# A sort on one core: the product of the last payload columns goes from VectorE to GpSimd, and bucket one-hots are made two steps sooner

## What is computed

```python
h = emb
acc = emb
for _ in range(LAYERS):                       # 2
    h = jax.ops.segment_sum(adj_val[:, None] * h[adj_col], adj_row, num_segments=N)
    acc = acc + h
graph_item_embs = acc / (LAYERS + 1)
...
scores = select @ _l2norm(graph_item_embs).T
```

## Time and profile before

| | us |
|---|---|
| median of 3 runs | 3988.06 (3985.89 to 3988.77) |
| the profiled execution | 3990.2 |
| its span | 3988.2 (mean granted TensorE clock 0.794) |
| busy over the span: PE / PEld / DVE / ACT / POOL | 2638.1 / 2222.1 / 3011.5 / 830.1 / 2657.9 |

### The profile page before, as it was taken

The page is one execution under the profiler, slowest core; times in us unless marked ns, Lnnn a source line. Parts: engine busy times, 40 slices in busy tenths (PEclk is TensorE's granted clock), DMA queues, the critical chain, the costliest instruction groups (busy, mean ns, idle before and its releaser), DMA issues.

```text
span 3988.2 us, 79764 instructions
## 1 busy us (share of the span) xinstructions
PE 2638.1 (66%) x14097; PEld 2222.1 (56%) x14098; DVE 3011.5 (76%) x7238; ACT 830.1 (21%) x2728; POOL 2657.9 (67%) x2685
## 2 busy tenths in 40 slices
PE   4899889555566566566666556665556555565898
PEld 2676666455565555555555555555555555553454
DVE  8999999767777677777777677767677777677675
ACT  0999999200000000000000000000000000004554
POOL 1355555777777777777776777777777777775771
PEclk7899999777777776777778677778787787786999
DMA  1011111422222222222223222222222222234343
GB/s 37 3 4 3 3 3 3 110 53 54 55 54 54 54 55 55 55 55 55 55 55 103 62 55 55 56 56 56 56 55 55 55 55 55 54 81 140 95 139 139
DMA packets 165449, 228.71 MB, mean 57 GB/s; under 512 B 79020, under 2 KB 119084, under 8 KB 164908
## 3 DMA queue, kind: packets, MB, share of 16 engines
q0 software_dynamic: 102640, 162.39, 19.8%
q1 hardware_dynamic: 47856, 58.94, 4.8%
q10 hardware_dynamic: 14540, 3.70, 0.8%
HBM read 183.57 MB, written 41.35 MB: 56 GB/s over the span
## 4 chain that ended last, share of the span: by engine, by line
DMA 30%; POOL 27%; issue 19%; DVE 13%; PE 6%; ACT 2%; SPq 2%; ACTq 0%; DVEq 0%; POOLq 0%
POOL store L649 25%; DMA store<-in_L_rec_emb,store 16%; DMA store<-table,store 13%; PE bank L1707 2%; DVE store L1020 2%; DVE big L964 2%; PE bank L1650 2%; POOL store L676 1%; DVE store L972 1%; ACT big L723 1%; DVE big L980 1%; DVE big L1445 1%; SPq L496 1%; DVE store L1045 1%; DVE store L906 1%
## 5 line engine op out<-in xcount | busy, mean ns | idle before, releaser
L1650 PE MATMUL bank<-store,shared 128*128 x9792 | 1731.2, 351 | 1137.5 <-POOLq L634 790.5
L1650 PEld LDWEIGHTS bank<-store,shared 128*128 128x128 f32 x9792 | 1610.9, 258 | 1257.8 <-issue 1255.5
L1338 DVE TENSOR_TENSOR acc<-acc,bank 128x256 f32 x2448 | 1022.6, 418 | 799.7 <-PE bank L1650 780.5
L1288 DVE TENSOR_SCALAR shared<-bank,mlo,mval 128x256 f32<-128x256 f32 x2448 | 1324.0, 541 | 0.0
L649 POOL DMA_INDIRECT store<-in_L_rec_emb,store x1128 | 1065.4, 945 | 384.2 <-issue 326.0
L649 POOL DMA_INDIRECT store<-table,store x1128 | 1066.4, 945 | 370.0 <-issue 317.9
L739 ACT COPY mlo<-store 128x24 f32 (+1 forms) x102 | 21.5, 211 | 2793.0 <-PE bank L1650 1977.6
L723 ACT ACTIVATE big<-big 128x72 f32<-128x72 bf16 x1764 | 569.7, 415 | 0.0
L1550 PE MATMUL bank<-big,store 128*128 128x144 f32 x2352 | 480.2, 333 | 72.1 <-DVE store L972 17.3
L1550 PEld LDWEIGHTS bank<-big,store 128*128 128x128 f32 x2352 | 357.0, 206 | 192.8 <-ACT big L723 169.5
L604 POOL DMA_INDIRECT sorted_edges<-moved,block_to x167 | 311.2, 1863 | 57.1 <-issue 57.1
(11 more groups left out here) (265 smaller groups left out, 1439.4 us busy)
## 6 DMA issues: line engine op xcount, KB each, us to landing
store<-in_L_rec_emb ACTq DMA_DIRECT2D x3008, 0.5 KB
store<-in_L_rec_emb SPq DMA_DIRECT2D x3008, 0.5 KB
store<-table SPq DMA_DIRECT2D x3008, 0.5 KB
store<-table ACTq DMA_DIRECT2D x3008, 0.5 KB
scores<-store SPq DMA_DIRECT2D x48, 512.0 KB, 2.8
store<-in_L_rec_emb,store POOLq DMA_INDIRECT x1128
store<-table,store POOLq DMA_INDIRECT x1128
table<-acc SPq DMA_DIRECT2D x7, 896.0 KB, 10.6
```

What stands on the lines that cost most here:

```text
L1288: dve.tensor_scalar(onehot[:, u % SR, :], bank[7][:, 0:BUCKET], mlo[:, u:u + 1], mval[:, u:u + 1], ALU.is_equal, ALU.mult).then_inc(s_S[u ...
L1338: add = dve.tensor_tensor(acc[:, bass.ds(off, BUCKET)], acc[:, bass.ds(off, BUCKET)], bank[u % PR][:, 0:BUCKET], ALU.add)
L1650: last = pe.matmul(bank[u % PR][:, q * D:(q + 1) * D], onehot[:, u % SR, q * P:(q + 1) * P], msg_flat[:, bass.ds(offs[u], D)], start=True, ...
```

## The change

GpSimd takes over the product of the last columns, and now of three columns (CL = 5: columns 5, 6, 7), in all 147 steps: one product of 128 x 432 f32 per step. VectorE's product of two columns (128 x 288) goes, and ScalarE makes 5 columns, 10 activations, where it made 6. GpSimd's order is written out: in `scatter(g)`, the products of steps 2 to 6 of group g+1 come ahead of the scatters 1, 3, 4, 6 and 7; those of step 7 and of step 0 of group g+2 follow the ninth scatter, and that of step 1 of group g+2 follows the gate that waits for the landing. Ahead of the loop GpSimd makes the products of the whole first group and of two steps more. In the last full group's scatter the product of the very last step comes behind all 9 scatters. VectorE's `hot_columns` now also waits for GpSimd's product of four steps before, GpSimd's product for `hot_c` and for the free slot, and TensorE for GpSimd's product ahead of column 5.

Besides, `hot_buckets` is issued for the group after next at step 6 (it was for the next group at step 0), and TensorE's `edges_before` (line 1535) at step 6 for the group after next.

```diff
+    CL = CA - 1
+    BETWEEN = {1: 2, 3: 3, 4: 4, 6: 5, 7: 6}
...
+            def last_columns(g, s):
+
+                n, r = SG * g + s, s % Q
+                pool.wait_ge(s_hc, n + 1)
+                pool.wait_ge(s_pm, n + 1)
+                pool.tensor_tensor(at_c[:, r, CL:C, :, :],
+                                   hot_c[:, r, :, CL:C].rearrange("p n t -> p t n").unsqueeze(2).broadcast_to([P, C - CL, 2, LC]),
+                                   pays[:, bass.ds(n * C + CL, C - CL), :].unsqueeze(3).broadcast_to([P, C - CL, 2, LC]),
+                                   ALU.mult).then_inc(s_valg, 1)
+
+            def scatter(g, h, blocks=NK, skip=0, after=0):
...
                 for k in range(blocks):
+                    if after == 2 and k in BETWEEN:
+                        last_columns(g + 1, BETWEEN[k])
                     pool.indirect_dma_start(slots, bass.IndirectOffsetOnAxis(block_to[:, h, k:k + 1], 0),
...
+                if after == 2:
+                    last_columns(g + 1, SG - 1)
+                    last_columns(g + 2, 0)
+                elif after == 1:
+                    last_columns(g + 1, 2)
                 pool.wait_ge(s_free, g + 3)
                 pool.wait_ge(s_sct, 16 * (NK * g + blocks))
                 pool.tensor_tensor(gate[:, 2:3], gate[:, 1:2], gate[:, 1:2], ALU.add).then_inc(s_free, 1)
+                if after == 2:
+                    last_columns(g + 2, 1)
...
-            with pool.Fori(0, GR // 2) as i:
+            for s in range(SG):
+                last_columns(0, s)
+            last_columns(1, 0)
+            last_columns(1, 1)
+            with pool.Fori(0, GR // 2 - 1) as i:
                 for h in range(2):
-                    scatter(2 * i + h, h)
+                    scatter(2 * i + h, h, after=2)
+            scatter(GR - 3, 0, after=2)
+            scatter(GR - 2, 1, after=1)
             scatter(GR - 1, 0, NKL, FIRST)
...
-                for t in range(CA):
+                for t in range(CL):
...
                 dve.wait_ge(s_val, CA * n + CA)
+                ge(dve, s_valg, n - Q + 1)
...
-            def last_columns(g, s):
-
-                n, r = SG * g + s, s % Q
-                dve.wait_ge(s_hc, n + 1)
-                dve.tensor_tensor(at_c[:, r, CA:C, :, :],
...
                 for s in range(SG):
-                    if s == 0 and hot is hot_b:
-                        hot_buckets(g + 1)
-                    elif s == 3:
+                    if s == 6 and early:
+                        hot_buckets(g + 2)
+                    if s == 3:
                         edges_before(g + 1)
...
-                    last_columns(g, s)
...
-                    if t < CA:
+                    if t < CL:
                         pe.wait_ge(s_val, Q * CA + CA * n + t + 1)
-                    elif t == CA:
-                        pe.wait_ge(s_valv, n + 1)
+                    elif t == CL:
+                        pe.wait_ge(s_valg, n + 1)
...
             edges_before(0, kept[:, 0])
+            pe.wait_ge(s_rk, 1)
+            edges_before(1, kept[:, 1])
...
                     permute(g, s, h, SG)
-                    if s == 0:
-                        edges_before(g + 1, hot)
+                    if s == 6 and hot is not None:
+                        edges_before(g + 2, hot)
                     elif s == 4:
                         bucket_steps(g)
```

More of the change, by code:

```diff
@@ L380, in recommender_program @@
         s_val = sem("s_val")
-        s_valv = sem("s_valv")
+        s_valg = sem("s_valg")
         s_pm = sem("s_pm")
@@ L598, in opened @@
                 pool.tensor_tensor(gate[:, 0:1], gate[:, 1:2], gate[:, 1:2], ALU.add).then_inc(s_gate, 1)
-            def scatter(g, h, blocks=NK, skip=0):
+            def last_columns(g, s):
[7 more added lines that the diff above has]
+            def scatter(g, h, blocks=NK, skip=0, after=0):
                 opened(g, [(s_gev, g + 3), (s_to, g + 2)])
                 for k in range(blocks):
+                    if after == 2 and k in BETWEEN:
+                        last_columns(g + 1, BETWEEN[k])
                     pool.indirect_dma_start(slots, bass.IndirectOffsetOnAxis(block_to[:, h, k:k + 1], 0),
@@ L724, in payloads @@
                                               scale=what[:, bass.ds(n * C + t, 1)])
-                    last.then_inc(s_val, 1)
+                    last.then_inc(s_val, 1 + CA - CL if t == CL - 1 else 1)
             with act.Fori(0, GR // 2) as i:
@@ L974, in hot_partitions @@
                                   ALU.is_equal).then_inc(s_hp, 1)
-            def last_columns(g, s):
-                n, r = SG * g + s, s % Q
-                dve.wait_ge(s_hc, n + 1)
-                dve.tensor_tensor(at_c[:, r, CA:C, :, :],
-                                  hot_c[:, r, :, CA:C].rearrange("p n t -> p t n").unsqueeze(2).broadcast_to([P, C - CA, 2, LC]),
-                                  pays[:, bass.ds(n * C + CA, C - CA), :].unsqueeze(3).broadcast_to([P, C - CA, 2, LC]),
-                                  ALU.mult).then_inc(s_valv, 1)
             def edges_before(g):
@@ L1078, in targets, with sort_group @@
                 dve.tensor_tensor(block_to[:, h, 0:blocks], bank[7][:, 0:blocks], number[:, :], ALU.add).then_inc(s_to, 1)
-            def sort_group(g, h, width=LC, hot=hot_b):
+            def sort_group(g, h, width=LC, hot=hot_b, early=True):
                 for s in range(SG):
-                    if s == 0 and hot is hot_b:
-                        hot_buckets(g + 1)
-                    elif s == 3:
+                    if s == 6 and early:
+                        hot_buckets(g + 2)
+                    if s == 3:
                         edges_before(g + 1)
@@ L1148, in _ @@
             for g in range(KEPT - 1):
-                sort_group(g, g % 2, LC, kept[:, g + 1])
+                sort_group(g, g % 2, LC, kept[:, g + 1], g + 2 >= KEPT)
             with dve.Fori(KEPT // 2, GR // 2 - 1) as i:
@@ L1153, in _ @@
             sort_group(GR - 3, 0)
-            sort_group(GR - 2, 1, LCL)
+            sort_group(GR - 2, 1, LCL, early=False)
             dve.wait_ge(s_lat, 3)
@@ L1159, in _ @@
                 hot_partitions(GR - 1, s, 0)
-                last_columns(GR - 1, s)
                 if s == 0:
@@ L1567, in _, with sort_group @@
             edges_before(0, kept[:, 0])
-            def sort_group(g, h, hot):
+            pe.wait_ge(s_rk, 1)
+            edges_before(1, kept[:, 1])
+            def sort_group(g, h, hot=hot_b):
                 for s in range(SG):
                     permute(g, s, h, SG)
-                    if s == 0:
-                        edges_before(g + 1, hot)
+                    if s == 6 and hot is not None:
+                        edges_before(g + 2, hot)
                     elif s == 4:
@@ L1578, in _ @@
             for g in range(KEPT - 1):
-                sort_group(g, g % 2, kept[:, g + 1])
-            with pe.Fori(KEPT // 2, GR // 2) as i:
+                sort_group(g, g % 2, kept[:, g + 2] if g + 2 < KEPT else hot_b)
+            with pe.Fori(KEPT // 2, GR // 2 - 1) as i:
                 for h in range(2):
-                    sort_group(2 * i + h, h, hot_b)
+                    sort_group(2 * i + h, h)
+            sort_group(GR - 3, 0)
+            sort_group(GR - 2, 1, None)
             for s in range(LAST):
```

## The result

The changed kernel takes **4037.18 us** (median of 4 runs, 4034.49 to 4037.64) against 3988.01: **1.0123 times as long, 95% interval 1.0105 to 1.014**. I had forecast 3972.5 with a range of 3938 to 4013. The profiled execution took 4034.49 us.

The account below looks back on a forecast made before the run. VectorE was taken to bound the sort at 32.86 us a group, then GpSimd at 32.0 after the change: -14.6 us for 17 groups, -4 at the start, +3 at the end, -15.6 in all, 3972.5 us, range 3938 to 4013.

Parts of the forecast that it names:

- VectorE's term for the shared read: VectorE in the sort: waits for GpSimd's reads add 3.0 us a group to 28.2, making 31.2.
- Its own work: VectorE's work per sort group without its product and count waits: 28.2 us, from 32.86.
- The product's price: GpSimd's product of 432 elements in the sort: 1.25 us each, eight make 10.0 a group.
- the two estimates from the Trainium skill: GpSimd's product by the skill's pages: 1.13 or 1.49 us, the group 31.1 or 33.9 us.
- GpSimd as the bound: GpSimd bounds the sort after the change, at 32.0 us a group, VectorE 0.8 under it.
- ScalarE is no bound: ScalarE in the sort: 80 activations a group instead of 96 leave 26 us.
- Buckets sooner: Earlier bucket one-hots in the sort remove VectorE's waits for TensorE's counts: 6.4 us over 17 groups.
- Start: Up to the first opening gate: -5.8 from VectorE's ten steps and 1.8 of stalls, -4 us.
- The end: After the last group's late third product: first codes 6 us late, the rest 3 us late, +3 us.
- Slower: Rival: GpSimd's queue in the sort bounds above the old bound, from 1.36 us a product; 4012 us, chance 0.28.
- fast: Rival: VectorE still bounds the sort, at its lower work, with cheap products; 3949 or 3928 us, chance 0.18.
- Mutual waits: Rival: GpSimd and VectorE hold each other off in the sort; group 32.8 us, 3986 us, chance 0.12.

Follow-up runs that it names:

- a_fence: The changed kernel with a one-element GpSimd fill, and a wait for it, ahead of each of the six products that follow a scatter: 3965.39 us, ratio 0.9949.
- d_read: The kernel before plus five unused GpSimd products per group, behind scatters 0, 2, 3, 5 and 6: 4047.96 us, ratio 1.0154.
- d_idle: The kernel before plus five unused GpSimd products per group, in a row behind the landing gate, where no scatter runs: 4012.1 us, ratio 1.0064.
- hot_early: The kernel before with only the bucket one-hots and TensorE's counts two steps sooner: 3983.2 us, ratio 0.9985.
- b_last: The kernel before with one unused semaphore declared last of all: 3990.74 us, ratio 1.000.
- f_tail: a_fence with the last group's third product behind the first scatter of the last full group, not behind all nine: 3956.74 us, ratio 0.9918.
- b_sem: The kernel before with one unused semaphore declared ahead of those of the gather rounds: 3973.61 us, ratio 0.996.
- a_sem: The changed kernel with one unused semaphore where a_fence has its own, without fences: 4023.74 us, ratio 1.008.

## Why the prediction was wrong

**The step that failed is VectorE's term for the shared read**, 28.2 + 3.0 = 31.2 us. Its own work was right: 28.2 + 6.8 of measured holds = 35.0, which is its busy time a group (594.86 / 17); the last 0.6 of the 35.57 is its idle time. The prediction sized the holds at less than half, for two reasons. *The length of one*: it let a read wait for at most a product, 1.25 us. The rows show holds of 2.2, since a product already holds while it stands behind a scatter. a_fence takes away just that and wins 58 us, 3.4 a group, nearly the 3.8 that the term was short; the holds that it leaves, 2.8 a group, are about the 3.0 forecast. *How many*: it took products and reads as meeting by chance. They meet by schedule. The products wait for VectorE's own one-hots and are placed between scatters that run at one pace, so the same lines are hit in each group: line 1073 takes 2.38 to 2.44 us in 17 of its 19 runs.

Under both lies a premise of the text ahead of the prediction, that the engines "meet only at semaphores". d_read has no semaphore between its products and VectorE, and VectorE lost 4.3 us a group by them.

A third thing was missing: line 1073 (1054 before) reads one SBUF operand, and so was in no sum of the prediction. Held 2.1 us on average, it is the largest single item, 38 of the 122 us. The Trainium skill's same section of "SBUF — State Buffer" ("Who interferes with whom") warns of it: a `tensor_scalar` can enter a two-port mode, and then contends with GpSimd. The trace shows the contention (0.185 to 2.28 us), not the mode.

**The product's price** was a little high: 1.11 us for 1.25, so the strided operand cost little: a product of packed constants takes 1.06 (d_idle, 5.29 for five). The select's rate in the sum is 1.52 ns by its two rows and not 1.56, which moves the price by 0.02 us. Of the two estimates from the Trainium skill the lower, 1.13, came close; the surcharge for wide steps of its page "GPSIMD Engine Reference", section 7 (1.49 with it), did not show in 1.11.

**GpSimd as the bound**: wrong for the change (gate idle 34.8 us), right for the fenced kernel, where 32.0 forecast stands against 32.20. That nearness is in part luck: the fenced kernel has six fences a group that the sum has not (in the rows of a_fence the product starts at 599.14, 0.46 us behind the scatter's end at 598.68; the sum has 0.1), and its products are cheaper than priced.

**ScalarE, hot buckets, start, end.** ScalarE is no bound, as said. Buckets sooner: 6.4 forecast, 6.7 us in hot_early. Start -5.9 for -4: 1.8 of stalls had been added, and the gate came 5.9 sooner, near what VectorE's ten steps alone give (5.8); but b_last, whose sort is the same as before, has that gate 1.0 sooner too. The end +10.3 before and -5.6 after the first gather, +4.7 for +3: behind TensorE's last step the chain to line 1278 took 25.2 us (761.65 to 786.85) and not 21.1. In f_tail, undoing the late product alone, the last full group's gate to the first gather is 35.6 us again.

**The rivals.** *Slower* had the right sign and the wrong mechanism: it needed a product above 1.36 us, and it was 1.11. By the same 1.11 the *fast* rival should have won: VectorE did bound, as it says, but not at its lower work. *Mutual waits* named the cause and gave it 0.8 us a group more, 32.8; it was 35.57. The prediction says that no row shows a VectorE operation held by GpSimd, and let one last a product at most. What a trace doesn't show was here the whole result. The kernel before could not show it, for GpSimd ran nothing there but one-element sums and scatters. A bound with each of the six products that follow a scatter holding a read for both, and the other two for themselves, 6 x (1.55 + 1.25) + 2 x 1.25 = 19.3 us a group, would have put the range's end far above 4013.

## What to carry to other kernels

Work moved to an idle engine can be paid by the bounding one, where the two hold up each other's reads: count the bounding engine's reads that can stand behind the new instructions, each for such an instruction and for what is left of a scatter ahead of it, and look at the bounding engine's *mean durations* after the change, not at its idle time. Behind a scatter, one small write and a wait ahead of a reading instruction can be worth more than they cost. And where a variant declares a semaphore more, run the kernel before with that semaphore too, or 15 us of nothing can pass for a gain.

## What was not expected of the hardware

- A product on GpSimd (both operands in SBUF) that stands behind a running scatter already holds VectorE's reads: 2.2 us of hold by a product of 1.11 us, 2.05 in d_read; with the fence at most 0.99, in d_idle at most 0.76.
- VectorE's one-operand line 1073 (f32, 64 wide) is held as the two-operand ones are: 0.185 to 2.28 us. So is line 1099 in a_fence (`begun_buckets`, 0.80 us, up to 1.79).
- Adding one unused semaphore ahead of those of the gather rounds shortens these by 13 to 17 us of 2880 (b_sem, a_sem), declared last it does nothing (b_last). From 740 to 3500 us, the gathers' waits for earlier gathers' data are 35.6 and 22.3 us in b_sem, against 49.9 and 30.4 before. Why other semaphore numbers do that stays open; nothing was tried beyond these runs.
- That the hold spans the scatter rests on durations and on the fence's gain. A product ahead of a product does not extend it so (d_idle, five in a row, 0.76 us); other instructions were not tried.
